# Experts' first product among the last shared ones, x ahead of the moves for two tiles, a reordered end, expert weight pieces spread anew, the condition loaded by ScalarE

## The chip, the core and the metric

One core of a Trainium2 chip. The metric is the device time of one execution in microseconds (us). The engines in the rows are PE (TensorE matmul; PEld is its weight load), DVE (VectorE), ACT (ScalarE), POOL (GpSimd) and SP (SyncE, which here only starts DMAs). A name with a q behind it (ACTq, SPq) is that engine's instruction queue where it issues DMAs.

## What is computed

Two layers in float32 over 4096 tokens of 512 channels: a modulated linear with a residual, and a mixture of experts with one shared part and two routed experts for each token.

```python
ys = y * scale
d = rsqrt(einsum('bi,io->bo', ys * ys, weight * weight) + EPS)
x = x + einsum('bsi,io->bso', x * ys[:, None, :], weight) * d[:, None, :]

shared = silu(xf @ w1) * (xf @ w3) @ w2                  # 512 -> 1024 -> 512
s = sigmoid(concat([xf, tf]) @ router_W)                  # 8 experts
topk_idx = top_k(s + router_bias, 2); gates = s_sel / (s_sel.sum() + 1e-9)
h = gelu(einsum('nc,ech->enh', xf, W1e))                  # each token: its 2 experts
routed = combine(gates, einsum('enh,ehc->enc', h, W2e))
x = x + (shared + routed) / 3
```

## The kernel before

Every product is made of three matmuls on fp32r parts: high by high, high by low, low by high. A "high" is a copy to fp32r by ScalarE, a "low" the rest by VectorE. So each operand passes ScalarE, then VectorE, before PE may use it.

**Stages.** First the linear over 8 blocks of 512 tokens (`first_linear`, `linear`), ahead of which PE runs 20 matmuls on zeros. Then 8 shared blocks (0 to 7) of 8 steps (`hc`): `up(n, hc)` has 24 matmuls, and `down(n, hc-1)` 12. Behind `up`, ScalarE makes silu (`gate`, tile `sil`), VectorE the gated product `gm`, ScalarE `gh`, VectorE `gl`; `down` needs `gl`. In the first step of a block VectorE also adds the residual of the block before (`output`, tile `outst`), and `down(n, 0)` in the second step waits for that. Then the routed part: 71 tiles of 128 rows, sorted by expert.

**Tiles.** The rows of a tile lie in `xs_d` in DRAM, put there by GpSimd during blocks 2 to 7 (`put_row`, an indirect DMA for each 128 rows). `turn_x` (VectorE) transposes, `x_high_of` (ScalarE) and `take_x` (VectorE) split, `matmul1` multiplies (12 matmuls), `hidden` is gelu by ScalarE, `move_h` is four DMAs that ScalarE issues to turn the hidden tile (`hid` to `hturn`), `turn_h` (VectorE) transposes the rest, `h_high_of` (ScalarE, tile `hidth`) and `take_h` (VectorE) split, and `matmul2` (12 matmuls) follows `matmul1` by LAG = 3 tiles. `take_y` scales by the gate, and GpSimd adds the rows into `out` by an indirect DMA (`scatter`). `scatter(t)` waits until `scatter(t-2)` has landed. PE looks up a tile's expert in the middle of the tile before (`look_up`).

**What sets the order.** There is no scheduler: each engine runs its instructions as written, and semaphores join them. On ScalarE a turn of a tile is: high of x for tile t+1, `hidden(t)`, `move_h(t)`, `h_high_of(t-2)`.

**Expert weights.** During blocks 0 to 5 the experts' weights are split as well, in 32 pieces. `piece_at(n, hc)` names the piece of a step. `move_piece` (SyncE) first waits until the piece before has been stored, then starts the load of the *next* piece into `eraw`, waits for the low part of this piece and stores it. `piece_high` (ScalarE, tile `ehl`) and `piece_low` (VectorE) split; both stand behind `gh` and `gl` in the step, and ahead of the next step's `sil` and `gm`. In step 5 of a block SyncE has, between pieces, `store_x1` and `load_x1t`. Before, blocks 0 and 1 have a piece in each step, blocks 2 to 5 one in each second step (0, 2, 4, 6). In block 1, VectorE also has the routing tables: `slot_rows` and `pad_rows` in step 6, `turns` and `tile_tables` in step 7. GpSimd starts on rows when these tables are done.

## Time and profile before

| | us |
|---|---|
| runs: median of three (lowest to highest) | 1148.37 (1056.49 to 2671.32) |
| the profiled execution | 1060.37 |
| its span, first to last instruction | 1058.6 |
| PE busy | 1031.7, 97% of the span |
| DVE, POOL, ACT busy | 505.7, 332.0, 292.0 |
| mean granted TensorE clock | 0.993 of full |

The profiled execution lies close to the lowest run, and all reckoning is against it. "Busy" of PE is the union of overlapping matmuls. An `[idle before <-X]` in a timeline is how long the engine stood still ahead of the row, and what released it.

### The profile page before, as it was taken

What the parts mean: (1) busy time and instruction counts of PE and PEld (TensorE: products, weight loads), DVE (VectorE), ACT (ScalarE), POOL (GpSimd) and SP (SyncE); (2) the same over time, 40 slices, a digit from 0 to 9 for tenths busy, and PEclk for the clock granted to TensorE, in tenths of its full rate; (3) what the DMA queues carried; (4) which work ended last, traced back from release to release, by engine and by line L of the source; (5) the groups of instructions that cost most, each with busy time, mean ns of one, the idle gap of its engine ahead of it and who ended that gap; (6) DMA issues with size and microseconds to landing.
All of it is one profiled execution on the core that took longest, in us unless ns stands there. A gap on an engine that the chain in (4) does not pass through costs nothing.

```text
span 1058.6 us, 14641 instructions
## 1 busy us (share of the span) xinstructions
PE 1031.7 (97%) x4712; PEld 842.4 (80%) x4712; DVE 505.7 (48%) x833; ACT 292.0 (28%) x461; POOL 332.0 (31%) x390
## 2 busy tenths in 40 slices
PE   9999999999999999999999998999999999999996
PEld 7888788787888888888888886788788787778874
DVE  4555556668323333243222215555555555555553
ACT  3222442322212212222121113332333233223321
POOL 0000000001223434343323301555455545545543
PEclk8999999999999999999999999999999999999998
DMA  5666688778877677886824777999779999999964
GB/s 171 199 215 223 239 285 260 261 274 278 273 238 263 193 268 241 264 276 201 291 79 108 211 226 193 218 226 221 152 139 191 225 220 226 221 219 222 230 120 80
DMA packets 133146, 228.61 MB, mean 216 GB/s; under 512 B 28912, under 2 KB 83840, under 8 KB 124992
## 3 DMA queue, kind: packets, MB, share of 16 engines
q1 hardware_dynamic: 60256, 144.05, 42.9%
q0 software_dynamic: 31360, 64.12, 26.7%
q10 hardware_dynamic: 41472, 19.68, 8.1%
q8 instruction: 35, 0.57, 0.2%
q14 instruction: 23, 0.19, 0.1%
HBM read 112.85 MB, written 98.38 MB: 200 GB/s over the span
## 4 chain that ended last, share of the span: by engine, by line
PE 69%; DMA 17%; issue 4%; DVE 4%; SPq 2%; POOL 1%; ACT 1%; ACTq 1%; POOLq 0%; DVEq 0%
PE banks L539 11%; PE banks L540 10%; PE banks L541 10%; PE banks L477 6%; PE banks L479 6%; PE banks L478 6%; DMA we_d<-ehl 6%; DMA we<-we_d 4%; PE banks L491 3%; PE banks L493 3%; PE banks L492 3%; PE banks L416 3%; PE banks L417 2%; PE banks L418 2%; DMA xs_d<-xrow,sadr 2%
## 5 line engine op out<-in xcount | busy, mean ns | idle before, releaser
L477 PE MATMUL banks<-xh,w 128*128 128x512 f32 x512 | 199.6, 390 | 0.6 <-DVE xl L738 0.6
L478 PE MATMUL banks<-xl,w 128*128 128x512 f32 x512 | 199.2, 389 | 0.0
L479 PE MATMUL banks<-xh,w 128*128 128x512 f32 x512 | 199.2, 389 | 0.0
L1200 POOL DMA_INDIRECT out<-ys,slot x71 | 124.6, 1754 | 187.2 <-DVE ys L1098 98.0
L807 DVE SCALAR_TENSOR_TENSOR gm<-sil,banks 128x512 f32<-128x512 f32 x64 | 43.9, 686 | 236.3 <-ACT sil L620 236.3
L1091 DVE TENSOR_TENSOR hidtl<-hidt,hidth 128x512 fp32r<-128x512 f32 x71 | 49.1, 692 | 173.8 <-ACT hidth L697 173.8
L539 PE MATMUL banks<-we,hidth 128*128 x284 | 113.6, 400 | 10.6 <-issue 9.0
L1186 POOL DMA_DIRECT2D xg<-xs_d x136 | 100.1, 1106 | 60.6 <-DVE xgt L1072 49.0
L620 ACT ACTIVATE sil<-banks 128x512 f32<-128x512 f32 x64 | 38.1, 595 | 281.8 <-PE banks L479 281.7
L539 PE MATMUL banks<-we,xgth 128*128 x284 | 111.3, 392 | 3.0 <-issue 3.0
L477 PEld LDWEIGHTS banks<-xh,w 128*128 128x128 f32 x512 | 96.1, 188 | 20.9 <-issue 1.1
L479 PEld LDWEIGHTS banks<-xh,w 128*128 128x128 f32 x512 | 96.1, 188 | 20.1
L478 PEld LDWEIGHTS banks<-xl,w 128*128 128x128 f32 x512 | 96.1, 188 | 19.8
L540 PE MATMUL banks<-we,hidth 128*128 x284 | 111.3, 392 | 0.0
L541 PE MATMUL banks<-we,hidtl 128*128 x284 | 111.2, 392 | 0.0
L541 PE MATMUL banks<-we,xgtl 128*128 x284 | 110.6, 389 | 0.0
L540 PE MATMUL banks<-we,xgth 128*128 x284 | 110.5, 389 | 0.0
L697 ACT ACTIVATE hidth<-hidt 128x512 fp32r<-128x512 f32 x71 | 44.9, 632 | 210.6 <-PE banks L541 108.9
L491 PE MATMUL banks<-wmh,gh 128*128 128x512 f32 x256 | 99.9, 390 | 3.1 <-DVE outst L819 3.0
L493 PE MATMUL banks<-wmh,gl 128*128 128x512 f32 x256 | 99.6, 389 | 0.0
L492 PE MATMUL banks<-wml,gh 128*128 128x512 f32 x256 | 99.6, 389 | 0.0
L1158 POOL DMA_DIRECT2D xrow<-padrows x1 | 0.6, 600 | 253.3 <-DVE place_of L1002 253.3
(173 smaller groups left out, 1519.1 us busy)
## 6 DMA issues: line engine op xcount, KB each, us to landing
we_d<-ehl SPq DMA_DIRECT2D x32, 1024.0 KB, 7.3
we<-we_d SPq DMA_DIRECT2D x48, 512.0 KB, 6.0
hturn<-hid ACTq DMA_DIRECT2D x284, 64.0 KB
xg<-xs_d POOLq DMA_DIRECT2D x136, 128.0 KB
eraw<-expert_w SPq DMA_DIRECT2D x32, 512.0 KB, 5.6
x1t_d<-x1t SPq DMA_DIRECT2D x8, 1024.0 KB, 8.8
xin<-x1t_d SPq DMA_DIRECT2D x8, 1024.0 KB, 9.0
x_d<-x1tok SPq DMA_DIRECT2D x32, 256.0 KB, 6.3
```

What stands on the lines that cost most here:

```text
L477: pe.matmul(ps[hc % 2][:, :], w_hi, xh[:, j, c, :], start=(c == 0), stop=False)
L478: pe.matmul(ps[hc % 2][:, :], w_hi, xl[:, j, c, :], start=False, stop=False)
L479: last = pe.matmul(ps[hc % 2][:, :], w_lo, xh[:, j, c, :], start=False, stop=(c == DC - 1))
L491: pe.matmul(o_ps[s][:, :], g_hi, w2h[:, hc, :], start=(hc == 0), stop=False)
L492: pe.matmul(o_ps[s][:, :], g_hi, w2l[:, hc, :], start=False, stop=False)
L493: last = pe.matmul(o_ps[s][:, :], g_lo, w2h[:, hc, :], start=False, stop=(hc == HC - 1))
L539: pe.matmul(ps, high[:, c, :], w_hi, start=(c == 0), stop=False)
L540: pe.matmul(ps, high[:, c, :], w_lo, start=False, stop=False)
L541: last = pe.matmul(ps, low[:, c, :], w_hi, start=False, stop=(c == DC - 1))
L1091: dve.tensor_tensor(hidtl[:, t % 2], hidt[:, t % 2], hidth[:, t % 2].bitcast(FP32), ALU.subtract).then_inc(hidt_done, 1)
L1186: pool.dma_start(xg[g * Q:(g + 1) * Q, m % 2 * PAIR:(m % 2 + 1) * PAIR].rearrange("p t a n -> p (t a) n"), xs_d[m * PAIR * P:(m + 1) * PAI ...
L1200: pool.indirect_dma_start(out[:, :], IO(slot[:, t, 0:1], 0), ys[:, t % RING, :], None, compute_op=ALU.add).then_inc(added[t % 2], 16)
```

## The change

Five parts, all of them order and place; no arithmetic is changed.

1. **Condition.** The DMA of `cnd` goes from GpSimd's queue to the head of ScalarE's.
2. **Pieces.** `piece_at` gives block 0 the steps 1, 3, 5, 7, block 1 the steps 0, 2, 3, 5, and blocks 2 to 5 the steps 0, 1, 3, 4, 6, 7. The DMA that zeroes the padding rows of `out` moves from block 1 to after block 5.
3. **First product.** PE runs `look_up(0)` ahead of the last `up`, and `matmul1(0)` between the last two `down`s. For that VectorE turns x of tiles 0 and 1 and makes the low part of tile 0 in step 6 of block 7, and ScalarE makes the high part of tile 0 ahead of the last `gate`. VectorE's `take_x(1)`, `take_x(2)` now stand ahead of `output(7)`. `hturn` and `hidth` change places, so that they don't lie where `xh` of block 7 or its residual still lie.
4. **x ahead of the moves.** For tiles 0 and 1, ScalarE makes the high part of tile t+2 ahead of `move_h(t)`.
5. **End.** `matmul1(70)` follows `matmul1(69)` at once; ScalarE's `h_high_of(68)` goes ahead of `move_h(70)`; VectorE's `take_y` goes behind `turn_h` and `take_h` from turn 70 on.

```diff
--- before.py
+++ after.py
@@ piece_at
     if isinstance(n, int) and n < 2:
-        half, m = HC // 2 * n, hc
-    elif hc % 2 == 0:
-        half, m = HC // 4 * (n + 2), hc // 2
+        steps, half = ((1, 3, 5, 7), (0, 2, 3, 5))[n], 2 * n
     else:
+        steps, half = (0, 1, 3, 4, 6, 7), 3 * n - 2
+    if hc not in steps:
         return None
+    m = steps.index(hc)
     return half * 2 + m, half + m // 2, half + (m + 1) // 2, m % 2
@@ the tiles
-        hturn = sb("hturn", [RING, SUB, P], FP32, 160)
+        hturn = sb("hturn", [RING, SUB, P], FP32, 128)
-        hidth = sb("hidth", [2, DC, P], FP32R, 132)
+        hidth = sb("hidth", [2, DC, P], FP32R, 160)
@@ sync
-                    if n == 1 and hc == 3:
-                        sp.dma_start(out[TOK:TOK + PADROWS, :], padrows).then_inc(pads_in, 16)
...
             load_weight(0, first[0], slice(0, 1))
+            sp.dma_start(out[TOK:TOK + PADROWS, :], padrows).then_inc(pads_in, 16)
@@ tensor
-            with pe.Fori(1, NBLK // 2) as h:
+            with pe.Fori(1, NBLK // 2 - 1) as h:
                 for j in range(2):
                     shared_block(2 * h + j, j)
+            shared_block(NBLK - 2, 0)
+            for hc in range(HC - 1):
+                up(NBLK - 1, hc, 1)
+                if hc:
+                    down(NBLK - 1, hc - 1)
+                else:
+                    down(NBLK - 2, HC - 1)
...
             pe.wait_ge(tables_done, 3)
+            look_up(0)
+            up(NBLK - 1, HC - 1, 1)
+            down(NBLK - 1, HC - 2)
             pe.wait_ge(gm_done, HC * NBLK - 1 + 2)
-            look_up(0)
+            matmul1(0)
             down(NBLK - 1, HC - 1)
             pe.wait_ge(gm_done, HC * NBLK + 2)
-            for t in range(TILES + LAG):
-                if t < TILES:
+            for t in range(1, TILES + LAG):
+                if t < TILES - 1:
                     matmul1(t)
+                if t == TILES - 2:
+                    matmul1(TILES - 1)
                 if t == LAG:
@@ scalar
+            act.dma_start(cnd[:, :, :], condT).then_inc(cond_in, 16)
             for c in range(DC):
                 act.dma_start(xin[:, 0, c, :], xT[0, :, c, :]).then_inc(x0_in[c], 16)
...
                 for hc in range(HC):
+                    if turn is None and hc == HC - 1:
+                        x_high_of(0)
                     gate(n, hc)
...
-                if hc == 1:
-                    piece_high(0, 0)
-                if hc:
-                    piece_high(0, hc)
+                piece_high(0, hc)
...
-            x_high_of(0)
+            x_high_of(1)
             for t in range(TILES + TURN_LAG):
-                if t + 1 < TILES:
-                    if t:
-                        act.wait_ge(mm1_done, t)
-                    x_high_of(t + 1)
                 if t < TILES:
                     hidden(t)
-                    if t == 0:
-                        act.wait_ge(o_done, SUB * NBLK)
+                if t < TURN_LAG:
+                    x_high_of(t + 2)
+                if t < TILES - 1:
                     move_h(t)
+                if t == TURN_LAG:
+                    act.wait_ge(o_done, SUB * NBLK)
                 if t >= TURN_LAG:
                     h_high_of(t - TURN_LAG)
+                if t == TILES - 1:
+                    move_h(t)
+                if TURN_LAG <= t < TILES - 2:
+                    x_high_of(t + 2)
@@ vector (piece_low(0, hc) changed as piece_high(0, hc))
+                    if n == NBLK - 1 and hc == HC - 2:
+                        turn_x(0)
+                        turn_x(1)
+                        take_x(0)
+            for t in range(2):
+                take_x(t + 1)
+                turn_x(t + 2)
...
-            turn_x(0)
-            turn_x(1)
-            take_x(0)
             output(NBLK - 1)
             for t in range(TILES + LAG + 1):
                 if t == 1:
                     dve.wait_ge(slots_in, 16 * SUB)
                     scatter_waits()
-                if t > LAG:
+                if LAG < t < TILES - 1:
                     take_y(t - LAG - 1)
-                if t + 1 < TILES:
+                if 2 <= t < TILES - 1:
                     take_x(t + 1)
-                if t + 2 < TILES:
+                if 2 <= t < TILES - 2:
                     turn_x(t + 2)
                 if 0 <= t - TURN_LAG < TILES:
                     turn_h(t - TURN_LAG)
                     take_h(t - TURN_LAG)
+                if t >= TILES - 1:
+                    take_y(t - LAG - 1)
@@ gpsimd
-            pool.dma_start(cnd[:, :, :], condT).then_inc(cond_in, 16)
```

VectorE at the border of steps 6 and 7 of block 1 (`padr` is the last of step 6's tables, `ehl` a weight piece, `gm` and `gl` are step 7's). Before:

```order
L941 TENSOR_SCALAR padtok<-tid 128x8 [waits step]
L942 CAST padr<-pad 128x8 [waits step]
L1009 TENSOR_TENSOR ehl<-eraw,ehl 128x1024 [waits eh_ready]
L807 SCALAR_TENSOR_TENSOR gm<-sil,banks 128x512 [waits sil_done]
L811 TENSOR_TENSOR gl<-gm,gh 128x512 [waits gh_ready]
L956 TENSOR_SCALAR o_107<-e_108 128x8
```

After:

```order
L956 TENSOR_SCALAR padtok<-tid 128x8 [waits step]
L957 CAST padr<-pad 128x8 [waits step]
L822 SCALAR_TENSOR_TENSOR gm<-sil,banks 128x512 [waits sil_done]
L826 TENSOR_TENSOR gl<-gm,gh 128x512 [waits gh_ready]
L971 TENSOR_SCALAR o_107<-e_108 128x8
```

The piece between the tables and step 7's gated product has gone; so has the one behind step 7's tables, ahead of block 2.

ScalarE from the last shared step into the tiles (`sil`, `gh`: shared; `xgth`: high of x; `hid`: gelu; `hturn<-hid`: the four DMAs of a move). Before:

```order
L625 ACTIVATE gh<-gm 128x512 [waits gm_done]
L676 ACTIVATE xgth<-xgt 128x512 [waits xturn_done] x2
L683 ACT_TABLE_LOAD
L683 ACTIVATE hid<-banks 128x4x4x32 [waits mm1_done]
L690 DMA hturn<-hid 32x4x128 [waits hid_done,o_done]
L690 DMA hturn<-hid 32x4x128 x3
L676 ACTIVATE xgth<-xgt 128x512 [waits xturn_done,mm1_done]
L683 ACTIVATE hid<-banks 128x4x4x32 [waits mm1_done]
L690 DMA hturn<-hid 32x4x128 [waits hid_done]
L690 DMA hturn<-hid 32x4x128 x3
L676 ACTIVATE xgth<-xgt 128x512 [waits xturn_done,mm1_done]
```

After:

```order
L658 ACTIVATE xgth<-xgt 128x512 [waits xturn_done]
L633 ACTIVATE sil<-banks 128x512 [waits ab_done]
L638 ACTIVATE gh<-gm 128x512 [waits gm_done]
L658 ACTIVATE xgth<-xgt 128x512 [waits xturn_done]
L695 ACT_TABLE_LOAD
L695 ACTIVATE hid<-banks 128x4x4x32 [waits mm1_done]
L658 ACTIVATE xgth<-xgt 128x512 [waits xturn_done]
L702 DMA hturn<-hid 32x4x128 [waits hid_done]
L702 DMA hturn<-hid 32x4x128 x3
L695 ACTIVATE hid<-banks 128x4x4x32 [waits mm1_done]
L658 ACTIVATE xgth<-xgt 128x512 [waits xturn_done]
L702 DMA hturn<-hid 32x4x128 [waits hid_done]
```

The first `xgth` went ahead of the last `sil`, and those of tiles 2 and 3 went ahead of the moves of tiles 0 and 1.

ScalarE's last instructions (`hidth`: high of the turned hidden tile). Before:

```order
L697 ACTIVATE hidth<-hidt 128x512 [waits mm2_done,hturn_done]
L683 ACTIVATE hid<-banks 128x4x4x32 [waits hturn_done,mm1_done]
L690 DMA hturn<-hid 32x4x128 [waits hid_done]
L690 DMA hturn<-hid 32x4x128 x3
L697 ACTIVATE hidth<-hidt 128x512 [waits mm2_done,hturn_done] x3
```

After:

```order
L709 ACTIVATE hidth<-hidt 128x512 [waits mm2_done,hturn_done]
L695 ACTIVATE hid<-banks 128x4x4x32 [waits hturn_done,mm1_done]
L709 ACTIVATE hidth<-hidt 128x512 [waits mm2_done,hturn_done]
L702 DMA hturn<-hid 32x4x128 [waits hid_done]
L702 DMA hturn<-hid 32x4x128 x3
L709 ACTIVATE hidth<-hidt 128x512 [waits mm2_done,hturn_done] x2
```

The `hidth` of tile 68 went ahead of the last tile's four DMAs; 69 and 70 stay behind them.

## Rows read from the trace of the kernel before

**Rows 1.** PE's waits in the whole span: for what, us in total, times, longest
```profile
PE banks L539 <- issue: 12.0, 22, 2.3
PE banks L491 <- DVE outst L819: 3.0, 2, 2.1
```

**Rows 2.** Windows: us, each engine's busy (x instructions), clock, DMA share, GB/s; block 3
```profile
310.00:376.00 66.00, 66.00 (x293) 54.66 (x292) 23.25 (x33) 16.21 (x25) 26.50 (x35) 1.00 0.71 236
```

**Rows 3.** Timeline of PE and DVE at the start: start, length, row, [idle before]
```profile
1.94 6.98 PE L460 MATMUL banks<-zeros 128*128 128x512 f32 x20 [1.94 <-DVE zeros L729]
9.48 1.16 PE L426 MATMUL banks<-xh,wmh 128*128 128x512 f32 x4 [0.56 <-ACT xh L584]
...
7.57 0.17 DVE L731 TENSOR_SCALAR mod<-cnd 128x16 f32<-128x16 f32 x1 [5.69 <-DMA cnd<-condT]
```

**Rows 4.** Line 587 (x, ScalarE's queue), then line 237 (w0, SyncE's queue)
```profile
L587 ACTq DMA_DIRECT2D xin<-xT x4: 402/450/502, 0.8 to 2.2; - x4
DMA to landing us min/median/max: 3.1/6.6/8.8
...
L237 SPq DMA_DIRECT2D w0s<-w x4: 391/426/432, 1.0 to 2.4; - x4
DMA to landing us min/median/max: 5.0/7.1/8.9
```

**Rows 5.** Timeline of PE, second steps of blocks 1 and 2
```profile
192.02 0.47 PE L491 MATMUL banks<-wmh,gh 128*128 128x512 f32 x1 [0.88 <-DVE outst L819]
...
260.58 0.50 PE L491 MATMUL banks<-wmh,gh 128*128 128x512 f32 x1 [2.10 <-DVE outst L819]
```

**Rows 6.** Timeline of ACT and DVE ahead of those two waits
```profile
185.10 1.06 ACT L640 ACTIVATE ehl<-eraw 128x1024 fp32r<-128x1024 f32 x1 [8.26 <-DMA eraw<-expert_w]
...
254.94 1.21 DVE L1009 TENSOR_TENSOR ehl<-eraw,ehl 128x1024 fp32r<-128x1024 f32 x1
...
258.05 2.48 DVE L819 TENSOR_TENSOR outst<-banks,xres 128x512 f32<-128x512 f32 x4
```

**Rows 7.** Timeline of PE, ACT and DVE between the shared blocks and the tiles
```profile
658.76 0.49 PE L539 MATMUL banks<-we,hidth 128*128 x1 [1.51 <-SPq L340]
...
645.55 2.63 ACTq L690 DMA_DIRECT2D hturn<-hid  x4
...
653.98 3.18 ACTq L690 DMA_DIRECT2D hturn<-hid  x4
657.21 0.63 ACT L697 ACTIVATE hidth<-hidt 128x512 fp32r<-128x512 f32 x1 [3.25 <-issue]
```

**Rows 8.** Timeline of PE, ACT and DVE in the last tiles
```profile
1040.93 0.79 PE L539 MATMUL banks<-we,hidth 128*128 x1 [2.27 <-issue]
...
1036.61 2.66 ACTq L690 DMA_DIRECT2D hturn<-hid  x4
...
1035.75 0.70 DVE L1085 STREAM_TRANSPOSE hidt<-hturn 128x512 f32<-128x512 f32 x1
```

**Rows 9.** Windows, as in rows 2, behind that wait
```profile
1040.90:1044.10 3.20, 3.17 (x8) 2.51 (x9) 1.79 (x3) 0.63 (x1) 1.55 (x1) 0.50 0.13 10
```

**Rows 10.** The last scatters on POOL (timeline), and landings of line 1200
```profile
1046.53 1.55 POOL L1200 DMA_INDIRECT out<-ys,slot  x1 [3.32 <-DVE ys L1098]
...
1053.41 1.55 POOL L1200 DMA_INDIRECT out<-ys,slot  x1 [2.59 <-DMA out<-ys,slot]
...
DMA to landing us min/median/max: 4.3/6.0/8.3
```

**Rows 11.** Block 3 (timeline of SP, ACT), and landings of line 302, 250 to 510
```profile
368.57 1.43 SPq L302 DMA_DIRECT2D eraw<-expert_w  x1
...
375.17 0.60 ACT L620 ACTIVATE sil<-banks 128x512 f32<-128x512 f32 x1 [5.23 <-PE banks L479]
...
DMA to landing us min/median/max: 3.2/7.6/11.2
```

**Rows 12.** POOL's waits, 255 to 610: for what, us in total, times, longest
```profile
POOL xrow L1136 <- DMA x_d<-x1tok: 21.8, 1, 21.8
```

21 lines of the change are left out of this document (9 added, 12 removed).

## Prediction

> **What bounds the kernel now.** I read the page's busy times first: PE is busy for 97% of the span, so only three things can shorten it: waits of PE, the stretch before its first useful matmul, and the stretch behind its last. The windows give PE's pace: block 3 of the shared part keeps PE busy for all of 66 us, with 293 matmuls of 512 columns at full clock, 0.225 us each [rows 2]. No part of the change removes a matmul. So I went to PE's waits in order: 12.0 us in 22 pieces ahead of the first matmul of a product of the tiles, and 3.0 us in two pieces for VectorE's `outst` [rows 1]. The rest of its idle time is the start and a tail behind its last matmul. All together PE is idle for 1058.6 - 1031.7 = 26.9 us, 2.5% of the span: the ceiling of any reordering. The timelines then say which of these waits the change touches.
>
> **The change, part by part.**
>
> *Condition.* PE's 20 matmuls on zeros run from 1.94 to 8.92, then it waits 0.56 us for `xh`, and starts at 9.48 [rows 3]. `xh` is late because `mod` needs the condition, which reached VectorE only at 7.57 [rows 3]. On ScalarE's queue the quickest of four DMAs landed in 3.1 us, and on SyncE's the first part of w0 in at least 5.0 from an issue at about 1.0, so w0 is there at 6.0 [rows 4]. With the condition first on that queue `mod` comes near 4, then w0 at 6.0 sets the first high parts, which end near 7.3, ahead of the zeros' end at 8.9. The x parts slip by one issue, 0.45 us [rows 4], which that slack hides. PE then waits for nothing: **0.6 us** saved (0.56 of idle and a little pipeline fill), at most 0.7, at least 0.
>
> *Pieces.* Two waits of PE hang on them. At 192.02 PE has waited 0.88 us, at 260.58 2.10 us, both for VectorE's `output` [rows 5]. The first goes back to ScalarE, which stood 8.26 us for a piece's load in step 7 of block 0, until 185.10, ahead of the next `sil` [rows 6]. In the new order the load issued in step 5 is that piece's, two steps ahead, so this wait goes. The second goes back to VectorE: the tables of block 1 fill it, a piece of 1.21 us starts behind them at 254.94, another stands between steps 6 and 7 (the order rows show both), and `output(1)` starts at 258.05 [rows 6]. Both pieces are gone there. That takes 2.4 us from a chain that is 2.10 late, so 0.3 us is left over. I take both waits whole: **3.0 us**. If the leftover is too little, 1 us comes back.
> What is late next: blocks 2 to 5 now have six pieces, not four. In block 3 the load behind SyncE's stores and `load_x1t` was issued at 368.57 [rows 11]. It used to be for the next block; now it is for step 7, whose `sil` is at 375.17 and whose piece is due some 2 us later, at 377.1. These loads land in 3.2 to 11.2 us, 7.6 in the median [rows 11], so at 371.8 to 379.8: ScalarE waits 0 to 2.7 us. In block 0 a wait of 8.26 cost PE 0.88 [rows 5, 6], so up to about 7 is free. I take 0 as the cost, with the other end in the rivals. The padding rows' DMA runs where the DMA engines are half idle, and nobody waits for it before the scatters: 0. Rows reach GpSimd's scatters sooner, as the tables end earlier.
>
> *First product and x ahead of the moves.* `matmul1(0)` now precedes the last `down`, 12 matmuls or 2.7 us earlier, and fills the small wait for `gl` there (0.24). All that tile 0 needs was done long before. Before, the first move started at 645.55 [rows 7]. Now it starts 2.9 earlier, but behind one more copy of 0.6: 643.2. It takes 2.63 as before. `matmul1(1)` ends 2.7 behind `matmul1(0)`'s old end less 0.24, so the second move starts at 645.55 + 2.7 - 0.2 + 0.6 = 648.6 and ends at 651.2. Gelu of tile 2 (0.6) and its move, 3.18 [rows 7], bring ScalarE to 655.1. There `hidth(0)` starts, where before it started at 657.21 [rows 7]: 2.1 us earlier. `matmul2(0)` waits for that (the row names SyncE, but `hidtl` follows `hidth` by about 0.7 and ends at that moment), so it starts at 656.7, not 658.76 [rows 7].
> PE runs `matmul1` of tiles 1, 2 and 3 without a break to 652.4, because x no longer waits behind moves. The waits that were spread between them collect ahead of `matmul2(0)`, as one idle stretch of 4.2 us where there was one of 1.51. In the last tiles PE stood idle for 2.27 us up to 1040.93 [rows 8], and the granted clock was 0.50, the level of 1.2 GHz, in the 3.2 us behind: 8 matmuls where 14 fit [rows 9]. That costs (14 - 8) x 0.225 = 1.4 us. The wait of 2.10 us in block 2 did not do it. So I expect the clock to fall here too. Half of that cost is hidden, since ScalarE's moves of over 3 us then set the pace anyway. Sum: 2.1 + 0.2 - 0.7 = **1.6 us** saved; 0.4 if the clock costs more, 3.5 if it doesn't fall and ScalarE's lead holds.
> The Trainium skill (TensorE: Matmul & The Clock Gate, "Why this matters for your kernels") warns against long idle gaps between bursts of matmuls, as the clock then falls to half. The trace agrees, with 0.50 behind an idle of 2.27 us; the rule speaks against this part of the change, which makes one long gap of several short ones.
>
> *End.* `hidt(68)` was turned from 1035.75 on, but ScalarE first issued the last move, 2.66 us from 1036.61, so PE waited 2.27 us until 1040.93 and then ran at half clock [rows 8, 9]. With `hidth(68)` ahead of the move that wait and the fall of the clock go: 2.3 + 1.4 = 3.7 on PE. `matmul1(70)` now comes 2.7 earlier than its x is ready by, some 0.7 late, but the later products have that slack. `ys(70)` comes 3 to 3.7 us sooner. But `scatter(70)` needs `scatter(68)` landed, and a scatter lands in 4.3 to 8.3 us [rows 10]. `ys(68)` stands behind `take_h(70)` now, so `scatter(68)` moves only from 1046.53 to about 1045.6, and `scatter(70)` from 1053.41 to no earlier than 1045.6 + 4.7 + 0.7 = 1051.0 [rows 10]. So **2.4 us** saved; 0.9 if the two keep their distance of 6.9, 3.7 if only PE counts.
>
> *Middle.* Of the 12.0 us of waits in the tiles, those of tiles 4 to 67 come where both orders are the same, row for row: 0.
>
> **The sum.** 0.6 + 3.0 + 1.6 + 2.4 = 7.6 us. Against the profiled execution's 1060.37 that gives 1052.8. The runs' lowest is 1056.49, which would give 1049; their median, 1148.37, and highest, 2671.32, are far above anything the trace holds, and nothing of the change bears on what did that. A measurement of this kernel can hardly tell less than 2%, 21 us, from no change.
>
> **Rivals.**
> *The gains as summed* (0.60): 1052.8, with a range of its own from 1047 (start, pieces, and the far ends 3.5 and 3.7) to 1058 (3.0 + 0.4 + 0.9 less 2 for scatter between runs).
> *No gain on balance, by DMA crowding* (0.18): two more pieces a block, each 0.5 MB in and 1 MB out, meet GpSimd's rows where the DMA share was already 0.71 [rows 2]. If loads behind `load_x1t` take as in block 0, each of blocks 2 to 5 gets a wait of 0.88 to 2.10 [rows 5], 3.5 to 8.4 us: 1056 to 1061, say 1059. For it: the landing of up to 11.2 [rows 11]. Against: the slack of some 7 us.
> *The clock and the scatters take the rest* (0.08): only start and pieces count, and the long idle stretch costs its full 1.4 with nothing hidden: 1060.4 - 3.6 + 1.4 = 1058. This is the rule cited above, told in this kernel's rows.
> *The order does not do what it says at the border* (0.04): if x of tile 0 is not ready in step 6 of block 7, VectorE's `turn_x(0)` holds up `gm`, `matmul1(0)` gains nothing, and the 1.6 becomes a loss of 1 to 3: 1056.
> *Slower* (0.05): GpSimd's rows slip. They end before the tiles with slack: GpSimd stood 21.8 us for block 7's tokens [rows 12], and `xg` was loaded some 20 us more ahead of its use. VectorE now waits for it 8 us earlier, ahead of the shared part's own products, and each microsecond past the slack is one of PE. From about 40 us of slip on it costs; at 70, 30% on each landing over some 230 us of scatters, it is 30 us: 1083, slower. The shares of rows 2 don't speak for so much.
> *More than all this* (0.05): the tiles' middle also settles, at most the 7 us left of rows 1: 1044.
>
> **How the numbers follow.** The likeliest case gives 1052.8. The range, 1046 to 1061, takes in its own, the crowding case, and the clock case, and leaves out the slow case, half of the case with more, and some of the scatter between executions. Faster by over 2% would need 1039 or less, beyond every case: 0.03. Slower by over 2% needs 1081.6: the slow case, and what the spread of the runs before may bring, 0.06. The rest, 0.91, is within 2%.
>
> **What would show it.** At the start, PE's first `wmh` matmul at 8.8 with no idle ahead of it. In blocks 1 and 2, no row of PE released by `outst`; in blocks 2 to 5, waits of ScalarE for `eraw` under 5 us and none of PE. Between blocks and tiles, `matmul1` of tiles 0 to 3 without a break, then one idle stretch of about 4 us ahead of the first `hidth` matmul and a clock of 0.50 behind it. At the end, no wait of PE over 1 us, and the last two even scatters 5 to 6 us apart. I am wrong if new waits of PE for `outst` or `gl` show in blocks 2 to 5, if `xgt` is late in block 7, or if the middle of the tiles has many more waits than before.

## The result, and the profile after

The changed kernel takes 1050.45 us, the median of 20 runs (1044.08 to 1061.56). The kernel before, run beside it, takes 1055.51 (20 runs; the lowest was 1049.72). The ratio of the changed kernel to the kernel before is 0.9962, interval 0.9946 to 0.9978: 4.0 us gained, between 2.3 and 5.7. The forecast was 1052.8, made of a base of 1060.37 and a gain of 7.6. Both were too large. The base, the profiled execution, lay 4.9 above the median that more runs of the kernel before gave. The gain was 2.5 us above the difference of the two medians (5.1) and 3.6 above the 4.0 of the ratio. So one error hides half of the other: that the forecast lies only 2.4 us from the measured time is in part luck. Single executions took far longer than the rest (up to 3678.63 us below); the medians include them, the ratios don't.

The profiled execution of the changed kernel has a span of 1044.4 us, 14.2 less than that of before, more than three times what the runs show. Most of the excess is the choice of the two executions: that of before lay 4.9 above the median of its kernel, that of the changed kernel (1046.31) 4.1 below its own. It helps to cut both spans at four events that every variant has: the first `up` matmul, the first matmul of the first expert product (used in the section on the experiments), and the start of the second product (`hidth`) of tiles 4 and 64.

| stretch of the span, us | before | after | gained | forecast |
|---|---|---|---|---|
| start to the first `up` | 113.5 | 112.0 | 1.5 | 0.6 |
| `up` to the second product of tile 4 | 568.7 | 562.3 | 6.4 | 4.6 |
| tile 4 to tile 64 | 337.1 | 332.0 | 5.1 | 0 |
| tile 64 to the end | 39.3 | 38.1 | 1.2 | 2.4 |

PE's waits of the changed kernel (for what, us in total, times, longest), to read against [rows 1]:
```profile
PE banks L546 <- issue: 6.9, 10, 2.2
PE banks L460 <- DVE zeros L744: 1.9, 1, 1.9
PE banks L477 <- DVE xl L753: 0.6, 1, 0.6
```
The two waits for `outst` are gone, and so is the one for `xh` at the start. What is left are the waits of the tiles, 6.9 us where there were 12.0 and 1.5.

**The start.** Timelines of PE and DVE of the changed kernel, to read against [rows 3]:
```profile
1.94 6.29 PE L460 MATMUL banks<-zeros 128*128 128x512 f32 x20 [1.94 <-DVE zeros L744]
8.07 1.07 PE L426 MATMUL banks<-xh,wmh 128*128 128x512 f32 x4
...
3.06 0.18 DVE L746 TENSOR_SCALAR mod<-cnd 128x16 f32<-128x16 f32 x1 [1.17 <-DMA cnd<-condT]
```
`mod` comes 4.5 us earlier, and no idle time stands ahead of the first useful matmul, as forecast. It starts at 8.07 rather than 8.8 because the 20 matmuls on zeros were 0.7 shorter in this execution.

**The pieces.** Window of block 3 of the changed kernel (columns as in [rows 2]):
```profile
310.00:376.00 66.00, 66.00 (x292) 54.67 (x292) 24.28 (x33) 17.22 (x26) 22.90 (x35) 1.00 0.84 288
```
Waits of its ScalarE between 250 and 510, and of its GpSimd between 255 and 610:
```profile
ACT ehl L653 <- DMA eraw<-expert_w: 16.3, 8, 4.0
...
POOL xrow L1155 <- DMA x_d<-x1tok: 7.4, 1, 7.4
```
The DMA engines are busier, 0.84 for 0.71, and ScalarE waits for a piece 8 times, 4.0 us at the longest, but PE misses none of it. GpSimd waits 7.4 us where it waited 21.8 [rows 12]: its rows lost time. In this execution they had it to lose; the section on first_h_early shows executions in which they had not.

**The border.** Timelines of PE and ACT of the changed kernel, for [rows 7]:
```profile
646.34 0.49 PE L546 MATMUL banks<-we,xgth 128*128 x1 [0.20 <-issue]
...
650.17 0.79 PE L546 MATMUL banks<-we,hidth 128*128 x1 [2.18 <-issue]
...
637.15 0.62 ACT L658 ACTIVATE xgth<-xgt 128x512 fp32r<-128x512 f32 x1
637.29 2.70 ACTq L702 DMA_DIRECT2D hturn<-hid  x4
...
642.73 2.52 ACTq L702 DMA_DIRECT2D hturn<-hid  x4
645.29 0.60 ACT L695 ACTIVATE hid<-banks 128x512 f32<-128x512 f32 x1 [2.08 <-PE banks L548]
645.92 2.60 ACTq L702 DMA_DIRECT2D hturn<-hid  x4
648.62 0.63 ACT L709 ACTIVATE hidth<-hidt 128x512 fp32r<-128x512 f32 x1 [2.73 <-issue]
```
Its windows around that wait:
```profile
647.60:650.20 2.60, 0.42 (x3) 0.03 (x1) 0.92 (x2) 1.58 (x3) 0.00 (x0) 0.99 0.74 174
650.20:654.00 3.80, 3.80 (x10) 3.04 (x11) 1.99 (x4) 1.12 (x3) 0.00 (x0) 0.56 0.57 188
```
The first products run on almost without a break (0.20), then PE stands 2.18 us for `hidth(0)`, which ScalarE could not start while it issued the four moves of tile 2, and behind it PE runs at half clock, 1.2 GHz: the window's mean is 0.56. The shape is that of the forecast, with an idle stretch of 2.2 us for the 4.2 worked out: counted from the first `up`, with 3.0 us for the pieces, the first products end when the step said, and `hidth(0)` comes 2 us sooner.

**The end.** Timelines of PE and POOL of the changed kernel, for [rows 8] and [rows 10]:
```profile
1018.85 0.49 PE L546 MATMUL banks<-we,xgth 128*128 x1 [1.55 <-issue]
...
1032.60 1.55 POOL L1218 DMA_INDIRECT out<-ys,slot  x1 [1.35 <-DVE ys L1118]
1035.74 1.55 POOL L1218 DMA_INDIRECT out<-ys,slot  x1 [1.59 <-issue]
1039.13 1.55 POOL L1218 DMA_INDIRECT out<-ys,slot  x1 [1.84 <-issue]
```
The idle stretch of 2.27 us ahead of the second product of tile 68 and the half clock behind it [rows 8, 9] are gone. In their place PE waits 1.55 us ahead of the first product of tile 70. The last two even scatters start 6.5 us apart, not 5 to 6.

### The profile page after: what moved, and what is told of

It reads as the page before. It is cut to its first block, busy times and chain, and to the rows that moved or that the text cites. A ratio compares the mean times of both kernels' runs of the same rounds, so it can differ in the third digit from the quotient of the medians.

```text
span 1044.4 us, 14564 instructions
## 1 busy us (share of the span) xinstructions
PE 1025.9 (98%) x4712; PEld 843.6 (81%) x4712; DVE 508.0 (49%) x833; ACT 292.8 (28%) x461; POOL 323.5 (31%) x389
## 4 chain that ended last, share of the span: by engine, by line
PE 97%; issue 1%; DMA 0%; DVE 0%; POOLq 0%; POOL 0%; ACT 0%; DVEq 0%; ACTq 0%
PE banks L546 12%; PE banks L547 12%; PE banks L548 12%; PE banks L477 11%; PE banks L478 11%; PE banks L479 11%; PE banks L492 6%; PE banks L493 6%; PE banks L491 6%; PE banks L416 3%; PE banks L417 2%; PE banks L418 2%; PE banks L454 1%; PE banks L460 1%; DMA out<-ys,slot 0%
## 5 line engine op out<-in xcount | busy, mean ns | idle before, releaser
L633 ACT ACTIVATE sil<-banks 128x512 f32<-128x512 f32 x64 | 38.3, 599 | 331.8 <-PE banks L479 331.8
L548 PE MATMUL banks<-we,hidtl 128*128 x284 | 111.2, 392 | 0.0
```

The costliest lines, as they stand in the source:

```text
L548: last = pe.matmul(ps, low[:, c, :], w_hi, start=False, stop=(c == DC - 1))
```

## The experiments

Every kernel below is the changed kernel with one edit, unless said otherwise; a minus in a diff is a line of the changed kernel. The question is twofold: does each part give what its step said, and where did the gain go that the profile shows and the runs don't? This table cuts the profiled execution of each as above (us), with the ratio of the runs to those of the kernel before.

| kernel | start to `up` | `up` to first expert product | to tile 4 | tile 4 to 64 | 64 to end | ratio (interval) |
|---|---|---|---|---|---|---|
| before | 113.5 | 528.4 | 40.3 | 337.1 | 39.3 | 1 |
| changed | 112.0 | 521.8 | 40.5 | 332.0 | 38.1 | 0.9962 (0.9946 to 0.9978) |
| same_again | 111.2 | 521.7 | 39.6 | 332.0 | 38.5 | 0.9986 (0.9954 to 1.0018) |
| undo_condition | 112.0 | 521.7 | 40.5 | 337.0 | 38.3 | 0.9944 (0.9910 to 0.9979) |
| undo_pieces | 112.4 | 525.9 | 41.9 | 332.7 | 38.5 | 1.0002 (0.9980 to 1.0023) |
| undo_border | 111.7 | 524.8 | 38.7 | 333.7 | 38.4 | 0.9966 (0.9938 to 0.9994) |
| undo_end | 112.2 | 521.7 | 42.9 | 341.3 | 38.0 | 0.9940 (0.9918 to 0.9962) |
| first_h_early | 111.2 | 521.7 | 42.1 | 336.5 | 38.6 | 0.9956 (0.9933 to 0.9979) |
| all_h_early | 112.4 | 521.8 | 40.1 | 330.1 | 36.6 | 0.9911 (0.9876 to 0.9946) |
| all_h_early_end | 111.2 | 521.8 | 37.5 | 326.9 | 37.4 | 0.9875 (0.9845 to 0.9904) |
| pair4_early | 111.6 | 521.7 | 41.9 | 337.0 | 39.2 | 0.9942 (0.9919 to 0.9965) |
| first_h_pair4 | 111.8 | 521.8 | 38.1 | 337.0 | 38.9 | 0.9933 (0.9909 to 0.9957) |
| all_h_end_pair4 | 112.0 | 521.7 | 37.5 | 333.2 | 37.2 | 0.9886 (0.9857 to 0.9915) |
| undo_end_pair4 | 111.2 | 521.7 | 41.3 | 332.0 | 37.6 | 0.9966 (0.9949 to 0.9983) |

The second stretch repeats to 0.1 us in all kernels that share its code. From there on one execution can't stand for its kernel: tile 4 to tile 64 takes 326.9 to 341.3 us. undo_condition, undo_end, pair4_early and the changed kernel have the same code there, and take 337.0, 341.3, 337.0 and 332.0.

**The same kernel once more (same_again).** No edit.

> The changed kernel unaltered, timed beside the others as their yardstick, and for a second look at what differs between executions. Theory A (the gains are fixed in place: start, blocks, border, end; the middle of the tiles only scatters between executions): PE's first wmh matmul near 8.1 to 8.8, no wait for outst, one idle stretch of 2 to 3 us ahead of the first second product with half clock behind it; the sum of PE's waits between second products 4 and 64 anything from 4 to 9 us. Theory B (the profiled execution is typical, and the middle of the tiles gained 4 us as well through the change): that sum again near 4.2 us, and a time near 1046.

1052.95 us. Its ratio lies 0.24% above the first measurement of the same kernel, and the intervals overlap. So nothing under some 3 us between two of these ratios is a finding here. The time, far from 1046, speaks for theory A, although the stretch from tile 4 to 64 took 332.0 us again: the profiled execution (1045.02) was again one of the quickest of its kernel. At the border the two profiles differ in one thing. Timeline of PE in same_again, and the window behind that row:
```profile
650.09 0.50 PE L546 MATMUL banks<-we,hidth 128*128 x1 [2.96 <-issue]
```
```profile
650.00:653.40 3.40, 3.31 (x15) 2.76 (x16) 1.71 (x3) 0.81 (x3) 0.00 (x0) 1.00 0.49 162
```
PE stands longer ahead of `matmul2(0)`, 2.96 us for 2.18, and the clock stays full behind it.

**The condition back on GpSimd's queue (undo_condition).**
```
-            act.dma_start(cnd[:, :, :], condT).then_inc(cond_in, 16)
+            pool.dma_start(cnd[:, :, :], condT).then_inc(cond_in, 16)
```


> The changed kernel with part 1 undone: the condition's DMA back on GpSimd's queue. Theory A: PE's first wmh matmul goes back to 9.5 us after an idle of 0.6 us or more, and the time is 0.6 to 1.5 us longer than the changed kernel's. Rival (the 1.4 us at the start came from the moment at which the clock rose, not from the condition): the first useful matmul stays under 8.6 in an execution in which the zeros end early, as it can't be, since mod needs the condition at 7.6; then the start differs by under 0.3 us.

1050.79 us. PE waits 1.4 us for `xh` again, and its first useful matmul starts at 9.56. Yet the first `up` starts at 111.98, as in the changed kernel (111.99). Shortly behind the demodulation, at about 20 us, PE's granted clock falls to half in every profile here, for 3.4 or for 6.8 us, and the difference between the two hides this term as long as one compares executions of different length there. Compared like with like it shows. With 3.4 us at half clock, the first `up` starts at 111.98 here and at 111.2 to 111.8 in the seven executions with the condition first. With 6.8 us, it starts at 113.48 in the kernel before and at 112.0 to 112.4 in the five others. So the stretch gains 0.2 to 0.8 us by the first pair and 1.1 to 1.5 by the second. A gain of the whole kernel is not shown (0.9944 without this part).

**The old order of the pieces (undo_pieces).**
```
-        steps, half = ((1, 3, 5, 7), (0, 2, 3, 5))[n], 2 * n
+        half, m = HC // 2 * n, hc
+    elif hc % 2 == 0:
+        half, m = HC // 4 * (n + 2), hc // 2
     else:
-        steps, half = (0, 1, 3, 4, 6, 7), 3 * n - 2
...
+                    if n == 1 and hc == 3:
+                        sp.dma_start(out[TOK:TOK + PADROWS, :], padrows).then_inc(pads_in, 16)
```


> The changed kernel with part 2 undone: pieces as before (each step of blocks 0 and 1, each second step of blocks 2 to 5), padding rows' DMA in block 1. Theory A: the two waits for outst come back, 0.9 and 2.1 us, the first up matmul of block 0 stays where it was, the first product of tile 0 starts 3.2 us later, and the time is 3 us longer. Rival (the new pieces' traffic costs in the row scatters and hides in the tiles): the waits come back but the time is less than 1 us longer.

1055.12 us, ratio 1.0002. Timeline of PE in undo_pieces:
```profile
191.18 0.47 PE L491 MATMUL banks<-wmh,gh 128*128 128x512 f32 x1 [1.12 <-DVE outst L837]
...
260.06 0.50 PE L491 MATMUL banks<-wmh,gh 128*128 128x512 f32 x1 [2.40 <-DVE outst L837]
```
Both waits are back, in the places of [rows 5], 1.12 and 2.40 us long. The stretch from `up` to the first expert product is 4.2 us longer. The kernel before, against undo_border, which has its order of the first product and the new pieces, gives 3.6 (528.4 to 524.8). This is the one part whose worth shows in a stretch that repeats. The runs agree: without it the median is back at that of the kernel before. But the interval (0.9980 to 1.0023) is only just clear of the first one of the changed kernel, and not of its repeat.

**The old border (undo_border).** The diff takes back `matmul1(0)` ahead of the last `down`, and ScalarE's and VectorE's x ahead of the moves.
```
             look_up(0)
...
-            matmul1(0)
...
-            for t in range(1, TILES + LAG):
+            for t in range(TILES + LAG):
...
-                    if turn is None and hc == HC - 1:
-                        x_high_of(0)
...
-                if t < TURN_LAG:
-                    x_high_of(t + 2)
```


> The changed kernel with parts 3 and 4 undone: first product of tile 0 behind the last down, x of tiles 2 and 3 behind the moves, tiles in their old places. Part 5 stays. Theory A: second product 0 starts 3.5 to 4 us later, but without the fall of the clock behind it, so that second product 4 starts 2.5 to 3 us later and the time is 2.5 us longer. Rival (what PE gains there is given back in the first tiles, since ScalarE's moves set the pace): second product 4 starts less than 1.5 us later, and the time is within 1 us.

1050.51 us, ratio 0.9966: by the ratios within 0.4 us of the changed kernel. Timeline of PE in undo_border:
```profile
640.03 0.49 PE L546 MATMUL banks<-we,xgth 128*128 x1 [0.60 <-issue]
...
644.59 0.50 PE L546 MATMUL banks<-we,xgth 128*128 x1 [1.09 <-issue]
...
648.44 0.49 PE L546 MATMUL banks<-we,xgth 128*128 x1 [0.41 <-issue]
...
653.12 0.49 PE L546 MATMUL banks<-we,hidth 128*128 x1 [1.06 <-issue]
```
The old order has several waits, none over 1.1 us, and no half clock here (1.00 from 25.1 us to 1042.3). The new one has one of 2.18 and then 3.4 us at half clock. So `matmul2(0)` starts 3.0 us earlier with the change (650.17 for 653.12), and four tiles later 0.9 is left of it (674.26 for 675.20).

**The old end (undo_end).**
```
-                if t == TILES - 2:
-                    matmul1(TILES - 1)
...
-                if t == TILES - 1:
-                    move_h(t)
...
-                if t >= TILES - 1:
-                    take_y(t - LAG - 1)
```


> The changed kernel with part 5 undone: tile 70's first product, the last hidth and the last ys in their old order. Theory A (the part's own gain is 2.4 us at the end of the span, 3.7 at the last matmul): PE waits 2 to 2.5 us ahead of second product 68 and runs 3.4 us at half clock behind it; from second product 64 to the last matmul it takes 3 to 4 us longer than in the changed kernel, to the end of the span 2.4 us. Rival (the scatters end the span anyway): the last matmul is 3 us later and the end less than 1.5 us.

1048.00 us, no slower than the changed kernel, although its profile lost most in the middle. From the second product of tile 64 PE needs 30.6 us to its last matmul, against 28.9 in the changed kernel and 31.8 before. To the end of the span it is 38.0 against 38.1. PE wins 1.7 us and the scatters keep them. The wait ahead of the second product of tile 68 is back (2.18 us up to 1040.17), but not the half clock behind it (last section).

**The rounding of the first gate tile's result ahead of the moves (first_h_early).** If `hidth(0)` is late only because it stands behind the four moves of tile 2, as the timeline of ACT above says, this takes the idle stretch away.
```
+                if t == TURN_LAG:
+                    act.wait_ge(o_done, SUB * NBLK)
+                    h_high_of(0)
                 if t < TILES - 1:
                     move_h(t)
...
-                if t >= TURN_LAG:
+                if t > TURN_LAG:
```


> The changed kernel with one instruction moved: hidth of tile 0 ahead of tile 2's move instead of behind it, so that the long idle stretch of PE ahead of second product 0 is gone. Theory C (the clock: what the sum promised and the median does not show went into TensorE at half clock, which this idle stretch starts): that stretch of 2 to 3 us is under 0.5 us, no half clock follows it, the mean clock of the runs rises from 0.992 by 0.0015 or more, and the time falls by 3 to 4 us, 2.2 for the wait and 1.6 for the clock. Rival D (ScalarE's turn sets the pace of the first tiles, so a stretch taken away there comes back as waits of the next second products): second product 0 starts 2.5 us earlier, second product 4 less than 1 us earlier, and the time is within 1 us.

1050.29 us. The cause holds: `matmul2(0)` starts at 646.81 (650.17), PE's largest wait there is 0.91, and the clock stays full. But the lead is gone by tile 4. Timelines of PE, DVE and SP in first_h_early:
```profile
675.03 0.49 PE L546 MATMUL banks<-we,hidth 128*128 x1 [4.05 <-issue]
...
672.13 0.71 DVE L1080 STREAM_TRANSPOSE xgt<-xg 128x512 f32<-128x512 f32 x1 [6.11 <-DMA xg<-xs_d]
...
638.08 16.36 SPq L335 DMA_DIRECT2D we<-we_d  x4
```
Its wait of POOL between 620 and 700, then SyncE's store of `out` in first_h_early and in all_h_early_end (below):
```profile
POOL xg L1205 <- DMA out<-outst: 23.0, 1, 23.0
...
658.24 0.39 SPq L281 DMA_DIRECT2D out<-outst  x1
...
652.23 0.39 SPq L281 DMA_DIRECT2D out<-outst  x1
```
VectorE waits 6.11 us for the rows of tile 8. GpSimd loads them only behind its wait for the last block's store of `out`. SyncE issues that store behind four weight quarters, each of which it waits for, 16.4 us in all. It is tempting to say that the earlier PE is, the longer it stands here: VectorE had no such wait before, and 1.3 us in the changed kernel. But all_h_early_end has its `matmul2(0)` just as early (646.80), and waits 1.0 us. What the wait goes with is the time of the store, and that goes with the time at which GpSimd's last rows have landed, for which SyncE waits before its first load of rows. The twelve profiled executions with the new pieces fall into two groups (us; the last column between 620 and 710):

| SyncE's first load of rows | last store of `out` issued | VectorE waits for rows | executions |
|---|---|---|---|
| 595.8 to 597.2 | 651.2 to 654.1 | 0 to 1.3 | changed, same_again, undo_border, all_h_early_end, pair4_early, undo_end_pair4 |
| 598.4 to 602.0 | 657.2 to 660.1 | 6.0 to 10.4 | undo_condition, undo_end, first_h_early, all_h_early, first_h_pair4, all_h_end_pair4 |

The instructions up to these loads are the same and in the same order in all of them, but for the condition's load in undo_condition (in undo_border two tiles lie elsewhere in memory). So the edits don't make the two groups. In the second group PE has one wait of 2.0 to 4.1 us between 674 and 690, and 3.4 us at half clock that begin within 1.5 us of its end. What delays the rows was not tested. The kernel before and undo_pieces, with the old pieces, load them at 601.8 and 601.6. They have no such wait, but their `matmul2(0)` starts only at 658.8 and 655.6.

**The same for every tile (all_h_early), and with the old place of the first product of tile 70 (all_h_early_end).**
```
-                if t < TILES - 1:
-                    move_h(t)
                 if t == TURN_LAG:
                     act.wait_ge(o_done, SUB * NBLK)
                 if t >= TURN_LAG:
                     h_high_of(t - TURN_LAG)
-                if t == TILES - 1:
+                if t < TILES:
                     move_h(t)
```
The second kernel has this besides, on PE:
```
-                if t < TILES - 1:
+                if t < TILES:
                     matmul1(t)
-                if t == TILES - 2:
-                    matmul1(TILES - 1)
```


> The changed kernel with hidth of tile t-2 ahead of the move of tile t for every tile, not for the last alone. ScalarE's four DMAs of 2.6 to 3.7 us then stand behind what PE waits for. Theory C: no idle stretch at the border, and the waits of PE between second products 4 and 64, 4 to 9 us before, are under 2 us; mean clock 0.995 or more; 7 to 10 us less than the changed kernel, 1041 to 1045 in the median. Rival D: hidth now waits for VectorE's turn of the tile, moves start 1 us later in each turn, and the waits move to the first products or to later hidth; the time is within 2 us of the changed kernel.

> As all_h_early, and PE's first product of tile 70 back behind second product 66. In the changed kernel PE stood 1.6 us for x of tile 70. Theory C: that wait goes, the last matmul comes 1 to 1.5 us earlier against all_h_early, the span ends 0 to 1 us earlier, since the scatters follow each other at their own pace. Rival D: as the last hidden tile is then turned one product later, second products 69 or 70 wait, and the end is 1 us or more later.

1043.83 and 1039.83 us, the latter 1.25% below the kernel before and the quickest kernel measured here. PE's waits in all_h_early_end:
```profile
PE banks L460 <- DVE zeros L740: 1.9, 1, 1.9
PE banks L546 <- issue: 1.0, 3, 0.5
PE banks L477 <- DVE xl L749: 0.6, 1, 0.6
```
Window of all_h_early_end over the border:
```profile
644.00:655.00 11.00, 10.52 (x44) 7.80 (x44) 4.93 (x9) 3.99 (x7) 0.00 (x0) 1.00 0.70 208
```
1.0 us of waits in all 71 tiles, where [rows 1] has 12.0, and full clock. That is the best of three executions: all_h_early has 4.3 us, 3.2 of them in one wait for late rows, and all_h_end_pair4 (below) 5.2, with one of 3.9. From tile 4 to 64, apart from that one wait, PE stands 0.1, 0.7 and 0.4 us in the three, and 2.4 to 6.8 in the others, always ahead of a second product. So most of PE's waits in the tiles, those in the middle included, were one thing: `hidth` behind four DMA issues on ScalarE's queue.

**The rows of tiles 8 and 9 ahead of GpSimd's waits.** Four kernels: the changed one (pair4_early), and first_h_early, all_h_early_end and undo_end with the same edit (first_h_pair4, all_h_end_pair4, undo_end_pair4).
```
             load_pair(3)
+            load_pair(4)
             pool.wait_ge(waits_done, 1)
...
-                if t % 2 == 0:
+                if t and t % 2 == 0:
                     load_pair(t // 2 + 4)
```


> The changed kernel with one move: GpSimd issues the row loads of tiles 8 and 9 ahead of its three waits (for the padding rows, the table of waits and the last block of out), where they stood behind them. Theory A (the lead won at the border is given back because these loads stand behind the store of the last block of out, which SyncE issues only after four weight quarters of 13.6 us): the loads are issued near 647 us instead of 658.5, VectorE's turns of x wait for no rows any more (1.3 us in the changed kernel's profile, 1.0 in its repeat, 6.9 with the condition load back on GpSimd), and the time falls by 1 to 4 us against the changed kernel's 1050 to 1053, to a ratio of 0.990 to 0.994 of the kernel before. Theory B (the lead goes into TensorE's clock, whatever becomes of the rows): the rows come early, the half clock behind the first second product stays (3.4 us at 650), and the time is within 1 us of the changed kernel, a ratio of 0.995 to 0.998. Theory C (the scatters' chain sets the end): the last tiles' second product comes earlier by what the rows gave, and the last scatter does not.

> The variant in which ScalarE's rounding of the first gate tile's transposed result goes ahead of its moves for tile 2 (time 1050.3, ratio 0.9956 when it was first run), with GpSimd's row loads of tiles 8 and 9 ahead of its waits besides. Theory A: in its first profile TensorE won 3.4 us at the first second product, and lost them at 672 us, where VectorE waited 10.4 us in all for these rows (longest 6.1); with the rows early that wait is gone, TensorE's idle stretch of 4.4 us ahead of the second product of tile 4 and the half clock at 676 are gone, and the time is 3 to 6 us below that of first_h_early: 1045 to 1047, ratio 0.989 to 0.992. Theory B (another release behind it is as late): the wait moves to SyncE's weights or the moves of hid, and the time is within 1.5 us of 1050.

> The quickest variant so far (every tile's rounding ahead of the moves, the order of the last tiles' first products as in the kernel before: 1039.8, ratio 0.9875) with GpSimd's row loads of tiles 8 and 9 ahead of its waits. Theory A: it had only 1.0 us of waits for rows in its profile, so it gains little from it: 1037 to 1040, ratio 0.985 to 0.988. Theory B (other executions than the profiled one waited longer for the rows, as with the condition load back on GpSimd): 2 to 4 us less, 1036 to 1038, ratio 0.982 to 0.985, with a mean granted clock above 0.996.

> The changed kernel with its new order of the last tiles undone (1048.0, ratio 0.994 in its first run, where it was quicker than the changed kernel although its profile lost 8 us more in the middle), and with the row loads of tiles 8 and 9 ahead of GpSimd's waits. It stands beside pair4_early, which differs from it only in the end. If the new order of the end is worth its 2.4 us of the forecast, this kernel is 2 to 3 us slower than pair4_early. If it is worth nothing, because the scatters of the last tiles set the end by then (38.1 us from the second product of tile 64 to the end of the span with the new order, 38.0 without), the two are within 1 us. If it costs something, this kernel is 1 to 3 us faster, as the first run hints.

1049.22, 1047.41, 1042.16 and 1050.62 us. Each interval overlaps that of its partner, and by the ratios the four differences go both ways (-2.1, -2.4, +1.2 and +2.7 us), so no gain of this edit is shown. The traces tell why. In pair4_early and undo_end_pair4 the store of `out` came early (652.9 and 651.2), so there was little to gain. In the other two it came at 660. Timelines of DVE and POOL in first_h_pair4:
```profile
683.50 0.71 DVE L1080 STREAM_TRANSPOSE xgt<-xg 128x512 f32<-128x512 f32 x1 [5.97 <-DMA xg<-xs_d]
...
666.00 1.69 POOL L1219 DMA_INDIRECT out<-ys,slot  x1 [12.20 <-DMA out<-outst]
674.56 1.58 POOL L1219 DMA_INDIRECT out<-ys,slot  x1 [6.86 <-DMA out<-ys,slot]
675.60 3.00 POOL L1205 DMA_DIRECT2D xg<-xs_d  x4
```
Tile 8's rows are early now, and the second product of tile 4 starts at 671.59, 3.4 us ahead of first_h_early (675.03). But the first scatter still waits for the store of `out`, and the rows of tiles 10 and 11 stand behind the first two scatters. So the same wait comes two tiles on, 5.97 us for 6.11. In all_h_end_pair4 it is 6.75 us, at 683.26. The theory was right on the place and wrong on the cure. The store itself, behind the weight quarters, would have to come earlier, or the rows of blocks 2 to 7; neither was tried.
In pair4_early the stretch of 2.18 us ahead of `matmul2(0)` was 3.5 us long instead, as ScalarE took 3.47 us over the moves of tile 2 (2.60 in the changed kernel), and the half clock lasted twice as long. That is the spread against which the times are to be held.
Between undo_end_pair4 and pair4_early the new order of the end is worth 2.5 us by the ratios, between undo_end and the changed kernel -2.3, with overlapping intervals both times: no worth shown in either direction.

## Where the prediction was right and where not

**Right:** the class, within 2%, and the likeliest case in its mechanisms. At the start `mod` comes early and no idle time is left. Both waits for `outst` hang on the pieces, and more DMA in blocks 2 to 5 costs PE nothing: the rival by crowding fell (PE busy for 66.00 of 66 us at a DMA share of 0.84). At the border came one idle stretch, then half clock. The slower case, rows that slip by 40 us and more, fell as well. But its mechanism was there in small: GpSimd's wait for block 7's tokens, 21.8 us before, was 7.4 in the changed kernel's profile and gone in undo_end, first_h_early and all_h_early. Where its last rows landed late, PE paid for it between 674 and 690, by way of SyncE's chain. The step had put this at nothing. That the denser pieces are what delays the last rows is likely from the lost slack, but no run shows it.

**Start, 0.6.** The idle time saved is as worked out, and 0.2 to 1.5 us of it are there at the first `up`, once executions with the same half clock behind the demodulation are compared. Whether it reaches the end could not be resolved: undoing this part did not slow the kernel.

**Pieces, 3.0.** Slightly small: the repeatable stretch gives 3.6 us (the kernel before against undo_border) to 4.2 (undo_pieces). It is the largest gain that is shown, and its possible price, the later rows, is not in it.

**Border, 1.6.** The step took 2.1 us for the start of `matmul2(0)`. Counted from the first `up`, it was 3.2 in the changed kernel against undo_border, and 2.6 in same_again. Two sizes were off. The moves of tile 2 took 2.60 us in the changed kernel (3.29 in same_again) for the 3.18 of [rows 7]. And 0.6 was added for the copy ahead of the first move, while ScalarE started that copy at 637.15 and the issue of the move at 637.29: that 0.6 was not paid. Then 0.7 was taken for the clock, half of the 1.4 of [rows 9]. From the first `up` to the second product of tile 4 it is 563.5 us in undo_border, 562.3 in the changed kernel, with the half clock, and 561.3 in same_again, without. So the part gives 1.2 or 2.2 us there, by the clock's luck, and 1.6 stands between them. Of the runs' time it gives nothing that shows: 0.9966 without this part, 0.9962 and 0.9986 with it.

**What is missing in the runs** shows in part in the mean granted clock of the unprofiled executions that the ratios use. It is 0.9950 to 0.9955 for the kernel before in its three series beside the experiments, which is 9 to 11 us at half clock, and 0.9927 and 0.9920 for the changed kernel and same_again (15 and 17 us). It is 0.9939 for undo_border (13), and 0.9955 for all_h_early_end (9, from four executions). Within a kernel, an execution with 1 us more at half clock took 0.5 us longer on average (a line through 203 executions, with much scatter). So each microsecond at half clock costs half a one where PE has work. It has none behind its last matmul, where the clock falls too: 4.1, 3.0 and 2.7 us of half clock lie there in before, undo_end and undo_end_pair4, and 4.5 to 6.9 in the nine profiles with the whole of part 5. So of the 5 to 7 us more, some 2 cost nothing, and the rest costs 1.5 to 2.5 us. The forecast had 0.7 for the clock in the whole change, where "half of it is hidden" was argued for one place only. Of the 3.6 us between the 7.6 summed and the 4.0 measured, this is 1 to 2.
Where the added half clock lies is known for profiled executions only. It lies behind `matmul2(0)` in the changed kernel and in undo_condition, undo_pieces, undo_end, pair4_early and undo_end_pair4, not in same_again, and not in undo_border. Further ones lie between 674 and 695 where rows were late. The seven kernels with the one long idle stretch have a mean of 0.9930, from 0.9913 to 0.9948, the six others with changed code 0.9940, from 0.9926 to 0.9955: by this the border's share is some 1 us of time. The other candidates for the rest are the end, and the late rows, which cost PE 2 to 4 us and the clock in six of twelve profiles. How often they are late in the other executions no run tells, so the account stays open there.
The Trainium skill (TensorE: Matmul & The Clock Gate, "Why this matters for your kernels") warned of long idle gaps between matmuls. The gaps of 2.18 and 2.27 us that were followed by half clock here are shorter than those that the page speaks of. The runs agree in direction: the mean clock of the kernels with the one long stretch is the lower one, though single kernels go the other way. They do not agree that a long gap alone decides (last section).

**End, 2.4.** Too large, and the largest single error: 1.2 in the profile (39.3 to 38.1), about nothing against undo_end (38.0). The step gave PE 3.7 and the scatters 2.4. PE won 2.9 from tile 64 to its last matmul (31.8 to 28.9), and the scatters kept the 6.5 us between the last two even ones (6.9 before). The low end of that term, 0.9 for a distance that stays, was the right one. The new wait for the x of tile 70 was put at 0.7 and said to be covered; it was 1.55.

**Middle, 0.** This failed as an account of one execution: the same code took 332.0 to 341.3 us. As the same rows of orders stood there, the step was right that the change adds nothing of its own, but wrong to take the profile's 7 us there as settled. In that stretch undo_condition's 5 us over the changed kernel are mostly one wait of 2.98 us behind late rows, with half clock behind it. pair4_early has eleven waits for `hidth` there, 6.0 us in all where the changed kernel has 2.8. The edit of all_h_early takes such waits away. That is also why the profile's 14.2 us was no measure of the change.

**Missed:** the chain that is late next. The forecast looked at GpSimd's slack for the first rows (`xg` ahead of its use) and not at the rows of tile 8, which have a release of their own: a store behind weight loads on another engine's queue, which themselves start when GpSimd's last rows have landed. In first_h_early that took back a lead of 3.4 us, in all_h_early_end, where the rows landed 4.5 us earlier, it did not.

**Two ends of the rivals do not follow from their terms.** 0.6 + 3.0 + 3.5 + 3.7 = 10.8 gives 1049.6, and 1047 only with over 2 us of scatter between runs besides. 1052.8 less the 7 us of the middle gives 1045.8 and not 1044. Neither bears on the forecast.

## What to carry to other kernels

Before moving work to an earlier place, follow the next loads that the faster engine will want, back through every queue that they stand in, and ask of each wait ahead of them whose it is: `load_pair(4)` stood behind a wait that only the scatter needed, and with that mended the next pair stood behind the scatter. Follow the chain to its first link, and look at that link in several executions before naming the cause: here it was the landing of rows at 596 or 602 us, long before the place where PE waited. An engine that both computes and issues DMAs should first issue what the bottleneck waits for: four issues in front of one rounding of 0.63 us cost more than all five parts of this change gave. By the ratios the three kernels that mend it are 5, 8 and 9 us below the changed kernel, which is 4.0 below the one before. And cut the span at events, and compare several executions: a gain counts where the stretch repeats (here to 0.1 us ahead of the tiles), and in the tiles only over many runs.

## What the runs showed of the hardware

**An idle stretch of one length sometimes costs the clock and sometimes not.** In the changed kernel, PE idle for 2.18 us up to 650.17 was followed by half clock, and 2.96 us at the same place of the same code in same_again was not. Window behind PE's idle stretch of 2.18 us up to 1040.17 in undo_end, then behind that of 2.14 us up to 1027.82 in undo_end_pair4:
```profile
1040.10:1043.50 3.40, 3.33 (x14) 2.75 (x15) 2.10 (x4) 0.63 (x1) 1.55 (x1) 1.00 0.24 16
```
```profile
1027.80:1031.20 3.40, 3.38 (x15) 2.81 (x16) 2.14 (x4) 0.63 (x1) 1.55 (x1) 1.00 0.21 17
```
Full clock both times, 14 and 15 matmuls in 3.4 us where [rows 9] has 8 in 3.2. The forecast took from [rows 8, 9] that such a stretch costs 1.4 us. In these rows it does so at times, and what decides was not found.

**Four DMA issues on ScalarE's queue have no fixed price.** The same four, of 64 KB each, took 2.5 to 4.9 us. The median move takes 2.6 in each kernel. For tile 2 it was 2.60 in the changed kernel, 3.47 in pair4_early, 3.86 in first_h_early, and the longest, 4.89 for tile 33 in undo_end, has one issue of 2.91. What lengthens them was not tested.

**A chain of loads that each wait for the one before varies as much.** SyncE's four weight quarters took 13.6 us in the changed kernel and 16.4 in first_h_early, and started at 635.2 and 638.1. The store of `out` that is queued behind them was issued at 652.6 and 658.2.
